# Batch-norm graph layer: statistics taken during the linear layer, and scale, linear layer or turning, and addition put in one stage by pieces

## What is computed

```
def _batchnorm(x, gamma, beta):
    mu = jnp.mean(x, axis=0)
    var = jnp.var(x, axis=0)
    return (x - mu) * jax.lax.rsqrt(var + EPS) * gamma + beta
...
agg = jnp.einsum('nm,bmd->bnd', A_hat, features)
x = agg.reshape(-1, d)
h = jax.nn.relu(_batchnorm(x @ W1.T + b1, g1, be1))
out = h @ W2.T + b2
out = _batchnorm(out, g2, be2)
return out.reshape(b, n, -1)
```

## Time and profile before

| what | value |
|---|---|
| median of 3 runs | 5671.01 us (5666.16 to 5678.43) |
| the profiled execution, its own time | 5673.73 us |
| span of the profiled execution | 5672.0 us |
| TensorE busy | 3660.9 us (65%) |
| VectorE busy | 3496.9 us (62%) |
| ScalarE busy | 1550.7 us (27%) |
| the five stages, first matmul to last addition | 3194.09 to 3323.55 us of the span |

### The profile page before, as it was taken

One profiled execution on the slowest core, in us unless ns is written; L12 is line 12 of the kernel. 1 busy time (PEld: TensorE's weight loads), 2 busy tenths in 40 slices (PEclk: granted clock), 3 DMA queues, 4 the chain that ended last, 5 costly groups with the idle time before them and its releaser, 6 DMA issues. The chain is left out here.

```text
span 5672.0 us, 68587 instructions
## 1 busy us (share of the span) xinstructions
PE 3660.9 (65%) x17454; PEld 2818.8 (50%) x17454; DVE 3496.9 (62%) x17858; ACT 1550.7 (27%) x3617; POOL 958.1 (17%) x1078
## 2 busy tenths in 40 slices
PE   6777764555933200026799456776969978968797
PEld 5666654444921100014476235774754545647575
DVE  6888888999889989964644343224343454433643
ACT  1111111120044410002343422223435434531343
POOL 0000000221022333200224005770000100000214
PEclk9999999999996555558899765557989999978899
DMA  3000000000000000000121021110000000000122
GB/s 97 1 1 1 1 1 1 20 1 1 0 1 1 1 1 1 1 0 2 28 74 41 2 33 9 9 9 2 0 17 1 0 9 0 0 4 1 32 79 61
DMA packets 137875, 76.98 MB, mean 14 GB/s; under 512 B 61196, under 2 KB 128742, under 8 KB 137062
## 3 DMA queue, kind: packets, MB, share of 16 engines
q1 hardware_dynamic: 108646, 53.21, 3.8%
q0 software_dynamic: 28928, 20.50, 1.9%
HBM read 42.67 MB, written 30.97 MB: 13 GB/s over the span
## 5 line engine op out<-in xcount | busy, mean ns | idle before, releaser
L1769 POOL DMA_INDIRECT e_sorted<-top_e_pair,top_e_pos x320 | 312.6, 977 | 1733.9 <-DVE top_e_pos L1645 1031.4
L2777 PE MATMUL l0g_tri_late<-l0g_tri_ya,l0g_tri_Z 128*128 128x2 f32 x762 | 199.6, 355 | 289.4 <-DVE l0g_tri_ya L2612 283.1
L2777 PEld LDWEIGHTS l0g_tri_late<-l0g_tri_ya,l0g_tri_Z 128*128 128x128 f32 x762 | 181.5, 319 | 313.6 <-DVE l0g_tri_ya L2612 306.7
L2049 POOL DMA_INDIRECT l1f_gas_rs<-l1f_ga_table_s,l1f_ga_slots x320 | 302.6, 946 | 113.8 <-issue 97.2
L957 PE MATMUL l0g_refz_tp<-top_ident,l0g_V 128*128 128x128 f32 x4 | 1.3, 440 | 478.9 <-PEq L3257 478.7
L3063 PE MATMUL l0g_val_sums<-l0g_val_sg,l0g_val_fold 128*128 128x156 bf16 x381 | 113.1, 312 | 285.5 <-DVE l0g_val_sg L3128 238.4
L2753 PE MATMUL l0g_tri_prod<-l0g_tri_Z,l0g_t_As 128*128 128x1 f32 x508 | 148.6, 362 | 147.9 <-DVE l0g_tri_Z L2693 128.1
L957 PEld LDWEIGHTS l0g_refz_tp<-top_ident,l0g_V 128*128 128x128 f32 x4 | 0.7, 194 | 479.4 <-issue 478.8
L2758 PE MATMUL l0g_tri_dots<-l0g_tri_Z 128*128 128x7 f32 (+31 forms) x762 | 215.4, 404 | 12.7
L3063 PEld LDWEIGHTS l0g_val_sums<-l0g_val_sg,l0g_val_fold 128*128 128x128 bf16 x381 | 39.6, 104 | 358.9 <-DVE l0g_val_sg L3128 309.6
L1747 PE MATMUL egl_hist<-egl_ohh,egl_ohl 128*128 128x64 bf16 x1568 | 206.4, 308 | 11.5 <-DVE egl_ohh L1713 11.1
(11 more groups left out here) (1042 smaller groups left out, 10635.6 us busy)
## 6 DMA issues: line engine op xcount, KB each, us to landing
e_sorted<-top_e_pair,top_e_pos POOLq DMA_INDIRECT x320, 2.1
l1f_gas_rs<-l1f_ga_table_s,l1f_ga_slots POOLq DMA_INDIRECT x320, 2.4
slot_rows<-l0g_t_nought SPq DMA_DIRECT2D x1, 4608.0 KB, 18.5
l0f_e_xs<-slot_rows SPq DMA_DIRECT2D x18, 256.0 KB, 3.2
slot_outs<-l0f_e_ys SPq DMA_DIRECT2D x18, 256.0 KB, 2.4
l3f_e_xs<-slot_rows SPq DMA_DIRECT2D x18, 256.0 KB, 3.0
slot_outs<-l3f_e_ys SPq DMA_DIRECT2D x18, 256.0 KB, 2.2
out_dram<-top_x SPq DMA_DIRECT2D x2, 2048.0 KB, 12.2
```

The costliest lines, as they stand in the source:

```text
L1769: nc.gpsimd.indirect_dma_start(out=g.sorted, out_offset=bass.IndirectOffsetOnAxis(ap=g.pos[:, j:j + 1].bitcast(U32), axis=0), in_=g.pair[: ...
L2049: nc.gpsimd.indirect_dma_start(out=rs[:, b, c, :], out_offset=None, in_=table_s, in_offset=bass.IndirectOffsetOnAxis(ap=slots[:, t, c, 0:1 ...
L2777: last = nc.tensor.matmul(late[:, 0:2], Z[:, b, h, 1 + 2 * J:2 + 2 * J].to_broadcast([P, P]), ya[:, h, r, :], start=(h == hs[0]), stop=(h ...
```

## The change

- `linear_T` gets an argument `stats`. Where it is given, VectorE takes the statistics of each piece in the same stage, as soon as ScalarE has written the piece (semaphore `moved`). The first linear layer uses it, and its statistics tile now lives in the layer.
- `batch_norm` takes its statistics as given. Its stage now also holds what followed. ScalarE applies scale and shift in instructions of 512 columns, by pieces (48 of them in both stages where there were 12 of 2048). TensorE waits for each piece (`applied`) and, in the first stage, multiplies it by W2; in the second it turns it. VectorE moves each piece out of the accumulator: in the first stage it adds the bias and writes aggT, which ScalarE did before, and takes the statistics of the piece before it for the second normalization; in the second stage it adds the piece to x.
- The stages "l1g_2" and "l1g_x" are gone: five stages are now three. What was in hardware loops in these two is now written out.

The diff:

```
--- before.py
+++ after.py
@@ -993,14 +993,25 @@
                                              func).then_inc(moved, 1)
 
 
-def linear_T(nc, g, tag, ins, W, outs, func, bias):
+def linear_T(nc, g, tag, ins, W, outs, func, bias, stats=None):
+
 
     K, M = len(ins), len(outs)
     with Scope(nc, tag) as s:
         acc = s.ps("acc", [P, 4, COLS])
         done, moved = s.sems("done", "moved")
         per = 4 // M
+        counted = s.sem("counted")
         with nc.Block() as block:
+            if stats is not None:
+                @block.vector
+                def _(dve):
+                    for i in range(NG):
+                        for m in range(M):
+                            dve.wait_ge(moved, 4 + i * M + m + 1)
+                            nc.vector.bn_stats(stats[:, m, i, :], outs[m][:, bass.ts(i, COLS)]).then_inc(counted, 1)
+                    dve.wait_ge(counted, M * NG)
+
             @block.tensor
             def _(pe):
                 pe.sem_inc(moved, 4)
@@ -1090,24 +1101,21 @@
                     last.then_inc(added, 1)
 
 
-def batch_norm(nc, g, tag, chunks, gamma, beta, func):
+def batch_norm(nc, g, tag, chunks, gamma, beta, func, stats, W=None, outs=None, bias=None, out_stats=None):
+
 
     M = len(chunks)
     with Scope(nc, tag) as s:
-        stats = s.sb("stats", [P, M, NG, 6])
         mv = s.sb("mv", [P, M, 2])
         std = s.sb("std", [P, M])
         sc = s.sb("sc", [P, M])
         sh = s.sb("sh", [P, M])
-        stats_done, aggr_done, std_done, dve_step, affine_ready, applied = s.sems(
-            "stats_done", "aggr_done", "std_done", "dve_step", "affine_ready", "applied")
+        acc = s.ps("acc", [P, 4, COLS])
+        aggr_done, std_done, dve_step, affine_ready, applied, done, moved, counted = s.sems(
+            "aggr_done", "std_done", "dve_step", "affine_ready", "applied", "done", "moved", "counted")
         with nc.Block() as block:
             @block.vector
             def _(dve):
-                for m in range(M):
-                    for i in range(NG):
-                        nc.vector.bn_stats(stats[:, m, i, :], chunks[m][:, bass.ts(i, COLS)]).then_inc(stats_done, 1)
-                dve.wait_ge(stats_done, M * NG)
                 for m in range(M):
                     nc.vector.bn_aggr(mv[:, m, :], stats[:, m, :, :].rearrange("p i k -> p (i k)")).then_inc(aggr_done, 1)
                 link = Chain(dve, dve_step)
@@ -1116,16 +1124,45 @@
                 link(nc.vector.tensor_tensor(sc[:, :], sc[:, :], gamma, ALU.mult))
                 link(nc.vector.tensor_tensor(sh[:, :], mv[:, :, 0], sc[:, :], ALU.mult))
                 nc.vector.tensor_tensor(sh[:, :], beta, sh[:, :], ALU.subtract).then_inc(affine_ready, 1)
+                if W is not None:
+                    for i in range(NG):
+                        dve.wait_ge(done, i + 1)
+                        nc.vector.tensor_scalar(outs[:, bass.ts(i, COLS)], acc[:, i % 4, :], bias, None, ALU.add).then_inc(moved, 1)
+                        if i > 0:
+                            dve.wait_ge(moved, i)
+                            nc.vector.bn_stats(out_stats[:, 0, i - 1, :], outs[:, bass.ts(i - 1, COLS)]).then_inc(counted, 1)
+                    dve.wait_ge(moved, NG)
+                    nc.vector.bn_stats(out_stats[:, 0, NG - 1, :], outs[:, bass.ts(NG - 1, COLS)]).then_inc(counted, 1)
+                    dve.wait_ge(counted, NG)
+                else:
+                    for i in range(NG):
+                        dve.wait_ge(done, i + 1)
+                        out = g.x[:, bass.ts(i, GRP), :]
+                        nc.vector.tensor_tensor(out, out, acc[:, i % 4, :].rearrange("p (k d) -> p k d", k=GRP), ALU.add).then_inc(moved, 1)
 
             @block.scalar
             def _(act):
                 act.wait_ge(aggr_done, M)
                 nc.scalar.activation(std[:, :], mv[:, :, 1], ACT.Sqrt, bias=g.eps5[:, :]).then_inc(std_done, 1)
                 act.wait_ge(affine_ready, 1)
-                for m in range(M):
-                    for i in range(NG // 4):
-                        y = chunks[m][:, bass.ts(i, 4 * COLS)]
+                for i in range(NG):
+                    for m in range(M):
+                        y = chunks[m][:, bass.ts(i, COLS)]
                         nc.scalar.activation(y, y, func, bias=sh[:, m:m + 1], scale=sc[:, m:m + 1]).then_inc(applied, 1)
+
+            @block.tensor
+            def _(pe):
+                for i in range(NG):
+                    pe.wait_ge(applied, (i + 1) * M)
+                    if i >= 4:
+                        pe.wait_ge(moved, i - 3)
+                    if W is not None:
+                        for k in range(M):
+                            last = nc.tensor.matmul(acc[:, i % 4, :], W[k], chunks[k][:, bass.ts(i, COLS)], start=(k == 0), stop=(k == M - 1))
+                    else:
+                        for k in range(GRP):
+                            last = nc.tensor.transpose(acc[:, i % 4, bass.ts(k, P)], chunks[0][:, bass.ts(i * GRP + k, P)], g.ident[:, :])
+                    last.then_inc(done, 1)
 
 
 def turned_adjacency(nc, g):
@@ -3678,11 +3715,11 @@
         aggregate_T(nc, g, "l1g_agg", xn, AhT, aggT, ACT.Copy)
         y = s.sb("y", [P, 2, TOK])
         halves = [y[:, 0, :], y[:, 1, :]]
-        linear_T(nc, g, "l1g_1", [aggT[:, :]], [W1T[:, :]], halves, ACT.Identity, v["b1"][:, :])
-        batch_norm(nc, g, "l1g_n1", halves, v["g1"][:, :], v["be1"][:, :], ACT.Relu)
-        linear_T(nc, g, "l1g_2", halves, [W2T[:, 0, :], W2T[:, 1, :]], [aggT[:, :]], ACT.Identity, v["b2"][:, :])
-        batch_norm(nc, g, "l1g_n2", [aggT[:, :]], v["g2"][:, :], v["be2"][:, :], ACT.Identity)
-        to_tokens(nc, g, "l1g_x", aggT, None, None, g.x, add=True)
+        stats1, stats2 = s.sb("stats1", [P, 2, NG, 6]), s.sb("stats2", [P, 1, NG, 6])
+        linear_T(nc, g, "l1g_1", [aggT[:, :]], [W1T[:, :]], halves, ACT.Identity, v["b1"][:, :], stats1)
+        batch_norm(nc, g, "l1g_n1", halves, v["g1"][:, :], v["be1"][:, :], ACT.Relu, stats1,
+                   [W2T[:, 0, :], W2T[:, 1, :]], aggT, v["b2"][:, :], stats2)
+        batch_norm(nc, g, "l1g_n2", [aggT[:, :]], v["g2"][:, :], v["be2"][:, :], ACT.Identity, stats2)
 
 
 def attention_routed_layer(nc, g, w):
```

## The result

The changed kernel takes 5624.66 us (median of 4 runs, 5621.26 to 5626.09), the kernel before 5672.2 us (5666.16 to 5678.43) in the same comparison. The ratio is 0.9915 with a 95% interval of 0.9898 to 0.9932: 47.5 us less, where 49.4 was forecast (5621.6 against 5624.66). The gain is clear of the scatter and under 1% of the whole. In a later comparison on its own chip the same pair came out at 5751.51 against 5800.44 us, ratio 0.9913 (0.9898 to 0.9929), 48.9 us less.

A forecast was written before the change was run, and what follows sets the result against it. The kernel was taken as a relay of five stages, each bound by one engine working alone. Gains of 18.4 + 15.2 + 8.4 + 7.4 = 49.4 us gave 5621.6 us from a 5671.0 median, range 5610 to 5636.

The forecast's parts named there:

- The first statistics: First linear layer: each statistic follows its piece's move, so joining begins at 3223.67 instead of 3242.05, 18.4 us less.
- Scaling by pieces: Ahead of the second linear layer: TensorE starts after two 512-column pieces, 1.55 us instead of 16.79, 15.2 us less.
- The Tanh row: Rejected price for 512-column scalings: a Tanh of 0.637 us implied a 0.55 us pace and 2 us more total gain.
- The matmuls: Second linear layer, first matmul to last move: TensorE stays owner at 1.72 us a piece, 29.90 us unchanged, zero gain.
- the cold start: Second linear layer: TensorE again starts at 1.2 GHz, an estimated 2.1 us lost; a warm start would gain that.
- The second statistics: Second layer's last move to second joining: only the last statistics show, 2.2 us instead of 10.61, 8.4 us less.
- Turning: Last stage, scaling, transposing and adding by pieces on three engines at once: 12.9 us instead of 20.29, 7.4 us less.
- the change of owner that was forecast: Turning stage: ScalarE sets the pace at 0.705 us a piece, against VectorE's 0.60 and TensorE's 0.63.
- The bounds of 5618 and 5624: Whole kernel: the forecast's own limits in us, 5618 standing for a warm start and cheap scaling.
- the clock at 1.2 GHz in the fused stages: Rival: waits between pieces keep TensorE's clock low, costing 24.5 us in matmuls and 2.9 in turning; 5649 us, chance 5%.
- That the pieces do not overlap: Rival: a wait keeps the new stages serial, only the statistics are hidden, 26.8 us less; 5644 us, chance 3%.
- A later layer at the lower clock: Rival: a later layer falls to 1.2 GHz, up to 5722 us; chance 2%, plus 2% for a loss looking like no change.

The follow-up runs named there:

- The trimmed kernel: Changed kernel plus unread matmuls heading the fused stages, turning-stage scalings of 512, 512, then 1024 columns, and last-statistic wait moved to the next block's head; 5749.61 us, ratio 0.9912.
- the two parts: Kernel before with only the statistics moved into the linear layers (5773.47 us, ratio 0.9951), or only the fused stages with statistics in their own pass (5779.48 us, 0.9958).
- the kernel with warming alone: Changed kernel plus matmuls that nobody reads, four at the head of the first fused stage and three in the second; 5754.51 us in a single run.

## Why the prediction was right

- **The first statistics**: 18.4 us forecast, 18.15 measured. A statistic beside ScalarE lasts 0.69 us instead of the 0.675 taken. The border was mis-sized: I took 0.30 us from the earlier trace rows, it is 0.54. The trimmed kernel shows where 0.22 of it are, in the wait for the engine's own last instruction. In the kernel before, the statistics and that wait both stood behind the barrier, so the earlier trace rows could not show it.
- **Scaling by pieces**: 15.2 forecast, 15.2 measured. The line through two sizes of the same form hit 0.797 us for one and 0.707 for the pace, and the run with 256 columns put a third point on it. The Tanh row would have given 0.55. The gain's stated bounds, 15.6 to 15.0, are a little wider than their own terms give: with a pace of 0.50 and of 0.80 us and a first scaling of 0.80 they are 15.4 and 15.1.
- **The matmuls**: 29.90 against 30.07. I had chosen the cold start, and it came: TensorE's records end at about 3224.5, the clock fell at about 3228 (0.78 over the window from 3226 to 3230), and the weight load at 3231.39 lasts 0.34 us. What it costs is shown by the trimmed kernel: 27.8 us for 30.07, 2.3 us where I had estimated 2.1. That the stretch came within 0.2 us of its old length is partly luck. In the other profiles that start cold it took 29.4 and 30.9 us (the two parts), 29.7 (the changed kernel again) and 30.3 (the kernel before again), by how soon the clock rises. VectorE's bias addition lasts 0.75 us, not the 0.69 of the nearest row; it was covered, except for the last one.
- **The second statistics**: 8.4 against 8.14, by the border (0.53 for 0.30) and by the last bias addition, after which the next statistic starts 0.66 us later and not 0.60.
- **Turning**: 7.4 against 7.45, with the change of owner that was forecast.
- **The sum**: 49.4 forecast, 48.8 in the stages; 49.3 between the spans of the two profiles, where losses ahead of the stages and gains behind them nearly cancel; 47.5 and 48.9 between medians. Of the 3.1 us by which 5624.66 lies above 5621.6, 1.2 are the kernel before, whose median went from 5671.01 to 5672.2 us with a fourth run. The bounds of 5618 and 5624 were too narrow by the runs' scatter, and the range with it held.
- **The rivals**: the clock at 1.2 GHz in the fused stages did not come, 1.00 from 3236 to 3260 us once the start was over; TensorE does not wait for pieces there. The Trainium skill, "TensorE: Matmul & The Clock Gate", section "A second HAM failure mode: psum-queue depth-cycling", tells of a kernel with bf16 matmuls whose clock swings because TensorE idles shortly between groups. This trace shows one rise, in float32 and without such idle times, so it does not test that rule. That the pieces do not overlap is refuted by the waits. A later layer at the lower clock was not seen: it would have cost microseconds behind 3277. The first pair of profiles gained 3.2 there, but 5.7 of the skip recurrences are in it, which are not the change's; the last pair, without that difference, gained 1.6.

## What to carry to other kernels

Where one engine after another owns a stage, price a fusion by the handovers: for each, the time from the last work of one owner to the first of the next, before and after. Then add the owner's own pace, and check each covered engine's work for one piece against it. Take the price of an instruction at a new size from a line through two sizes of the same form, since an engine with a fixed cost for each instruction can become the owner when pieces get small.

## What the runs showed of the hardware that was not expected

- **A wait for one's own last instruction ahead of a barrier** costs 0.22 us more than the same wait behind it (0.54 against 0.32 us of idle time, the same in both profiles of the trimmed kernel), and the instruction does not overlap with the barrier in either.
- **The clock can fall in the middle of warming.** In the kernel with warming alone the matmuls that nobody reads began at full clock, after 2.08 us of idle time in the first fused stage and 2.51 in the second; 1.4 and 0.2 us later the clock fell under them, and they delayed the real work. In the trimmed kernel they began 0.2 us earlier in each stage, after 1.86 and 2.30 us, and the clock stayed at 1.00 throughout, in both profiles. Since 2.30 us held and 2.08 did not, the length of the idle time alone does not tell which case comes. What does is open, and I would not count on the better one.
- **VectorE beside POOL.** In the kernel before, a VectorE multiplication of two SBUF operands took 6.04 us in the skip recurrences. The timelines of POOL and VectorE there:

```profile
4524.94 7.40 POOL L1260 COPY l2g_ls_xs<-l2g_hT 128x512 f32<-128x512 f32 x7 [6.65 <-DVE l2g_hT L1327]
```

```profile
4526.85 6.04 DVE L1316 TENSOR_TENSOR l2g_ls_cst<-l2g_ls_gt 128x512 f32<-128x512 f32 x1 [1.97 <-ACT l2g_ls_gt L1295]
```

  It ends 0.55 us after the seven copies in a row (4532.34), while its neighbours take 0.69 us. In the changed kernel's first profile the same seven copies last 8.78 us, and the instructions of VectorE beside them 0.80 to 1.63 us: the two engines seem to take turns there. This fits the Trainium skill, "SBUF — State Buffer", section "Terms", by which both engines share a pair of ports that one of them holds alone. No run here took the copies away, so it stays an explanation.
- **Comparisons differ by more than the change is worth.** The kernel before takes 5672 us in the first one and 5800 to 5802 in the three later ones. Between its two profiles the spans differ by 132.1 us, and 102.2 of them lie in one layer, where POOL gathers rows by indirect DMA: 440.9 us between the loads around it in the first profile and 543.1 in the second. It is 441 and 442 us in the first pair and 541 to 545 in all nine later profiles. There POOL waits 20 times for a VectorE instruction of that layer (line 2086), 102.2 us in all, and in the first profile never. The three later chips agree, and the first one's number is not recorded, so that the chip is the cause is not shown. The five stages agree to 0.7 us. So on the whole only runs of one comparison may be set side by side.
